# Attention scores in threes of adjoining PSUM banks, value products in cells of their own

## The reference, cut to what matters

```
x = x + linear_attention(_layernorm(x))   # 32 heads of 4, two decays, a scan over time, its own layer norm
x = x + ffn(_layernorm(x))                # 8 experts, all summed: silu(x @ wg) * (x @ wu) @ wd, 128 -> 512 -> 128
x = x + attention_b(_layernorm(x))        # 16 query heads of 8, one shared key/value head
x = x + ffn(_layernorm(x))                # the same weights again
```

```
att = einsum("bthd,bThd->bhtT", q, k) / sqrt(8)        # q, k after rotary tables
att = softmax(where(causal, -inf, att)); out = einsum("bhtT,bThd->bthd", att, v) @ Wo + bo
```

## Time and profile before

| | us |
|---|---|
| median of 3 runs | 1720.9 |
| the three runs | 1719.17, 1725.13, 1720.90 |
| the profiled execution | 1716.45 |
| its span | 1714.7 |

### The profile page before, as it was taken

The page is one execution under the profiler, slowest core; times in us unless marked ns, Lnnn a source line. Parts: engine busy times, 40 slices in busy tenths (PEclk is TensorE's granted clock), DMA queues, the critical chain, the costliest instruction groups (busy, mean ns, idle before and its releaser), DMA issues.

```text
span 1714.7 us, 24047 instructions
## 1 busy us (share of the span) xinstructions
PE 1574.8 (92%) x7848; PEld 1136.2 (66%) x7848; DVE 1169.0 (68%) x1943; ACT 892.6 (52%) x1552; POOL 723.4 (42%) x663
## 2 busy tenths in 40 slices
PE   3488998899999999899999999999999999999998
PEld 2266777677767676675665766767667667576676
DVE  5678787878787869676674755746647557466465
ACT  2255555464646464546445564464554644645554
POOL 3647354534444434311033544444344444343365
PEclk9689999999999999999999999999999999999999
DMA  6314543333334434333222332422323323333353
GB/s 196 111 41 162 192 160 115 148 135 144 127 148 148 148 119 147 140 111 111 111 101 85 126 128 85 146 102 107 138 92 130 117 107 115 118 111 117 111 191 117
DMA packets 36239, 216.71 MB, mean 126 GB/s; under 512 B 3475, under 2 KB 17300, under 8 KB 19732
## 3 DMA queue, kind: packets, MB, share of 16 engines
q1 hardware_dynamic: 36116, 215.18, 34.7%
HBM read 200.49 MB, written 15.47 MB: 126 GB/s over the span
## 4 chain that ended last, share of the span: by engine, by line
issue 29%; POOL 20%; PE 1%; POOLq 0%; DVE 0%; ACT 0%; DVEq 0%
POOL HL L525 18%; POOL QK L597 1%; POOL X L588 0%; POOL RSTD_f L516 0%; POOL RSTD_in L516 0%; POOLq L190 0%; PE bank L855 0%; PE bank L857 0%; PE bank L856 0%; POOL VE_f L513 0%; POOL VE_in L513 0%; POOL NB_in L520 0%; POOL NM_f L518 0%; POOLq L196 0%; POOL NM_in L518 0%
## 5 line engine op out<-in xcount | busy, mean ns | idle before, releaser
L525 POOL TENSOR_TENSOR HL<-HF,HH 128x512 fp32r<-128x512 f32 x312 | 417.4, 1338 | 657.7 <-ACT HH L689 657.7
L1233 DVE TENSOR_TENSOR HF<-SG,bank 128x512 f32<-128x512 f32 x512 | 349.5, 683 | 172.7 <-PE bank L857 103.6
L855 PE MATMUL bank<-XTH,W 128*128 128x512 f32 x1024 | 434.4, 424 | 10.4 <-ACT SG L682 9.9
L857 PE MATMUL bank<-XTH,W 128*128 128x512 f32 x1024 | 403.8, 394 | 0.0
L1216 DVE SCALAR_TENSOR_TENSOR SG<-SG,bank 128x512 f32<-128x512 f32 x288 | 197.9, 687 | 301.3 <-ACT SG L684 300.6
L856 PE MATMUL bank<-XTL,W 128*128 128x512 f32 x1024 | 403.1, 394 | 0.0
L684 ACT ACTIVATE SG<-bank 128x512 f32<-128x512 f32 x288 | 172.3, 598 | 399.4 <-PE bank L857 397.8
L689 ACT ACTIVATE HH<-HF 128x512 fp32r<-128x512 f32 x512 | 319.7, 624 | 28.4 <-DVE HF L1233 27.6
L682 ACT ACTIVATE SG<-bank 128x512 f32<-128x512 f32 x224 | 133.6, 596 | 245.7 <-PE bank L857 244.4
L855 PEld LDWEIGHTS bank<-XTH,W 128*128 128x128 f32 x1024 | 194.8, 190 | 91.6 <-issue 29.8
L855 PE MATMUL bank<-HH,W 128*128 128x512 f32 x512 | 216.8, 423 | 14.6 <-DVE HL L1222 13.4
(11 more groups left out here) (237 smaller groups left out, 1850.0 us busy)
## 6 DMA issues: line engine op xcount, KB each, us to landing
W<-kept_w SPq DMA_DIRECT2D x120, 1536.0 KB, 6.5
kept_w<-W SPq DMA_DIRECT2D x8, 1536.0 KB, 6.2
X<-in_L_attn_a_x_dram SPq DMA_DIRECT2D x8, 256.0 KB, 5.5
WS<-in_L_ffn_Wg_dram SPq DMA_DIRECT2D x8, 256.0 KB, 6.5
WS<-in_L_ffn_Wu_dram SPq DMA_DIRECT2D x8, 256.0 KB, 6.8
WS<-in_L_ffn_Wd_dram SPq DMA_DIRECT2D x8, 256.0 KB, 7.2
out_dram<-X SPq DMA_DIRECT2D x8, 256.0 KB, 7.2
CST<-in_tables_dram SPq DMA_DIRECT2D x1, 896.5 KB, 5.2
```

Source lines behind the costliest of these rows:

```text
L525: g.tensor_tensor(HL[:, n % HRING, :], HF[:, n % HFRING, :], HH[:, n % HRING, :].bitcast(F32), ALU.subtract).then_inc(F.hl, 1)
L855: pe.matmul(dst, wh, xh, start=start, stop=False)
L857: return pe.matmul(dst, wl, xh, start=False, stop=stop)
L1233: v.tensor_tensor(HF[:, n % HFRING, :], gated, fbank[(2 * n + 1) % 3], ALU.mult).then_inc(F.mul, 1)
```

## The change

The four side banks are now `three` (0, 1, 2, adjoining) and `abank` (3). The twelve units of scores of a sequence (a part and a group each; part 0 is the 128 by 128 block of all four heads of a group, parts 1 and 2 are 128 by 256 for two heads each) are taken in four threes, for rows as for columns; each unit fills one bank, so no bank is written by two row groups in one visit and `B.half` goes. A tile has 16 visits for 24, at alternating points 0 and 2. One Exp covers 1536 columns; PT holds the twelve banks of one sequence. The maxima are still six reductions a sequence, now of 512 to 1536 columns. Value products of a half are one cell with both parts. The FFN's ring of three banks is as it was. On ScalarE the Exp stands right behind the tanh, ahead of the HH copy; on VectorE maxima of visits at point 2 stand ahead of the doubled gate of the next slot. Cells of attention B get other slots and banks; its norm, turn and bias start five slots earlier, and statistics are at r = -21.

```diff
-ROW_PAIRS = [(0, 1), (2, 3), (4, 6), (5, 7), (8, 10), (9, 11)]
-PT_RING = 8
-B_CELL = {"turn": (-13, 1, 2), "q": (-8, 1, 0), "qs": (-8, 2, 1), "k": (-7, 1, 2), "ks": (-7, 2, 0), "v": (-5, 1, 0),
+B_CELL = {"turn": (-18, 1, 3), "q": (-8, 2, 0), "qs": (-7, 1, 1), "k": (-7, 2, 2), "ks": (-6, 1, 0), "v": (-5, 1, 1),
           "qst0": (-3, 1, 0), "qst1": (-3, 2, 1), "qst2": (-2, 1, 2), "qst3": (-2, 2, 0), "kst": (-1, 1, 1),
-          ("stack", 0, 0): (8, 1, 2), ("stack", 0, 1): (9, 1, 2), ("stack", 1, 0): (14, 1, 2),
-          ("stack", 1, 1): (15, 1, 2), ("sums", 0, 0): (20, 1, 2), ("sums", 0, 1): (21, 1, 2),
-          ("ot", 0): (22, 1, 2), ("out", 0): (23, 1, 2), ("sums", 1, 0): (27, 1, 2), ("sums", 1, 1): (27, 2, 1),
-          ("ot", 1): (28, 1, 2), ("out", 1): (29, 1, 2), "fturn": (33, 2, 2)}
-ROWS_AT = [[6 * b + i for i in range(6)] for b in range(SPT)]
-COLS_AT = [[12 + 6 * b + i for i in range(6)] for b in range(SPT)]
+          ("stack", 0, 0): (7, 1, 3), ("stack", 0, 1): (9, 1, 3), ("stack", 1, 0): (13, 1, 3),
+          ("stack", 1, 1): (15, 1, 3), ("pv", 0, 0): (16, 2, 3), ("pv", 0, 1): (18, 1, 3), ("sums", 0, 0): (20, 1, 3),
+          ("sums", 0, 1): (21, 1, 3), ("pv", 1, 0): (22, 2, 3), ("pv", 1, 1): (24, 1, 3), ("ot", 0): (25, 1, 3),
+          ("sums", 1, 0): (26, 1, 3), ("out", 0): (27, 2, 2), ("sums", 1, 1): (27, 1, 3), ("ot", 1): (28, 1, 3),
+          ("out", 1): (29, 1, 3), "fturn": (33, 1, 3)}
+ROWS_AT = [[(0, 2), (2, 0), (3, 2), (5, 0)], [(6, 2), (8, 0), (9, 2), (11, 0)]]
+COLS_AT = [[(12, 2), (14, 0), (15, 2), (17, 0)], [(18, 2), (20, 0), (21, 2), (23, 0)]]
+THREES = [[(0, 0), (0, 1), (0, 2)], [(0, 3), (1, 0), (1, 1)], [(1, 2), (1, 3), (2, 0)], [(2, 1), (2, 2), (2, 3)]]
+MAXIMA = [1, 3, 5, 6]
...
-            def exps(n, i):
-                m = 6 * n + i
-                act.wait_ge(B.t_ready, m + 1)
-                if m >= PT_RING // 2:
-                    act.wait_ge(B.pv, pv_of(m - PT_RING // 2))
-                act.activation(PT[:, at:at + 2, :], pair, ACT.Exp, scale=DB ** -0.5).then_inc(B.t_used, 1)
+                act.wait_ge(B.t_ready, 4 * n + i + 1)
+                after(act, B.pv, 2 * n)
+                act.activation(PT[:, 3 * i:3 * i + 3, :], three, ACT.Exp, scale=DB ** -0.5).then_inc(B.t_used, 1)
...
+                for at in range(0, 2 * SEQ, P):
+                    for x, (part, g) in enumerate(THREES[i]):
+                        if part == 0:
+                            pe.matmul(three[:, x, at:at + P], q[g][:, at // P, 0:P], ks[g][:, 0:P], start=(at == 0),
+                                      stop=False, skip_group_check=True)
+                        elif at % SEQ == 0:
+                            pe.matmul(three[:, x, at:at + SEQ], q[g][:, 2 * (part - 1) + at // SEQ, P:SEQ], ks[g],
+                                      start=(at == 0), stop=False, skip_group_check=True)
...
             def cols(t, b, i):
...
+                for x, (part, g) in enumerate(THREES[i]):
+                    rg = slice(g * RG, (g + 1) * RG)
+                    key = KST[rg, b * SEQ + P:(b + 1) * SEQ] if part == 0 else KST[rg, b * SEQ:b * SEQ + P]
+                    q2 = Q2[rg, b, :, P:SEQ] if part == 0 else Q2[rg, b, 2 * (part - 1):2 * part, :]
+                    pe.matmul(three[:, x, :], key, q2, start=True, stop=False, skip_group_check=True)
+                for x, (part, g) in enumerate(THREES[i]):
...
+            def values(n, b, z, dst):
+                pe.wait_ge(B.t_used, 4 * n + z + 3)
+                for g in range(NG):
+                    pe.matmul(dst[g * RG:(g + 1) * RG, :], VF[:, 2 * b, :], PT[:, NG * (z + 1) + g, :],
+                              start=True, stop=False, skip_group_check=True)
+                for g in range(NG):
+                    x = pe.matmul(r3(dst[g * RG:(g + 1) * RG, :], 2)[:, :, P:SEQ], VF[:, 2 * b + 1, :],
+                                  r3(PT[:, g, z * SEQ:(z + 1) * SEQ], 2), start=False, stop=True,
                                   skip_group_check=True)
...
+            def maxima(n, b, i):
...
+                for part in range(3):
+                    gs = [g for at, g in THREES[i] if at == part]
...
+                    v.tensor_reduce(dst, src, AX.X, ALU.max, negate=True).then_inc(B.row_used, 1)
...
+                new_maxima(slot, 2)
                 if n is not None and n >= TANH:
                     gated_half(n)
-                for t, r in b_tiles(slot):
-                    for b in range(SPT):
-                        if r in ROWS_AT[b]:
-                            maxima(t, b, ROWS_AT[b].index(r))
+                new_maxima(slot, 0)
```

More of the change, by code:

```diff
@@ L157, in side_cells, with put @@
     found = {}
[L159 to L162, removed]
+    def put(g, point, key):
+        bank = bank_of(key)
+        for at in range(3) if bank is None else (bank,):
+            assert (g, point, at) not in found, (g, point, at, key)
+            found[g, point, at] = key
     for t in range(NT):
[L164 to L167, removed]
+        for name, (r, point, _) in A_CELL.items():
+            put(a_slot(t) + r, point, ("a", t, name))
+        for name, (r, point, _) in B_CELL.items():
+            put(b_slot(t) + r, point, ("b", t, name))
@@ L830, in _ @@
                     gate_act(n)
+                for t, r in b_tiles(slot):
+                    for b in range(SPT):
+                        for i, (at, point) in enumerate(COLS_AT[b]):
+                            if r == at + (point == 2):
+                                exps(SPT * t + b, i)
                 n = unit_of(slot - 1)
@@ L970, in rows @@
                     pe.wait_ge(B.st_used, NJ * (t + 1))
[L971 to L978, removed]
-                                      stop=False, skip_group_check=True)
-                    for x in range(2):
-                        m = pe.matmul(r3(pair[:, x, :], NJ), MASKB[:, 2, :], spread(MASKB[:, 0, :], NJ), start=False,
-                                      stop=True, skip_group_check=True)
-                else:
-                    half = (units[0] - NG) % 2
-                    for j in range(2):
-                        for x in range(2):
-                            pe.matmul(pair[:, x, j * SEQ:(j + 1) * SEQ], q[x][:, 2 * half + j, P:SEQ], ks[x],
-                                      start=(j == 0), stop=False, skip_group_check=True)
-                    for x in range(2):
-                        m = pe.matmul(r3(pair[:, x, :], 2)[:, :, P:SEQ], MASKB[:, 2, :], spread(MASKB[:, 0, :], 2),
@@ L991, in rows @@
+                for x, (part, g) in enumerate(THREES[i]):
+                    if part == 0:
+                        m = pe.matmul(r3(three[:, x, :], NJ), MASKB[:, 2, :], spread(MASKB[:, 0, :], NJ),
+                                      start=False, stop=True, skip_group_check=True)
+                    else:
+                        m = pe.matmul(r3(three[:, x, :], 2)[:, :, P:SEQ], MASKB[:, 2, :], spread(MASKB[:, 0, :], 2),
                                       start=False, stop=True, skip_group_check=True)
@@ new lines, in cols @@
+                for x, (part, g) in enumerate(THREES[i]):
+                    if part == 0:
+                        m = pe.matmul(r3(three[:, x, :], NJ), MASKB[:, 2, :], spread(MASKB[:, 1, :], NJ),
+                                      start=False, stop=True, skip_group_check=True)
+                    else:
+                        m = pe.matmul(r3(three[:, x, :], 2)[:, :, 0:P], MASKB[:, 2, :], spread(MASKB[:, 1, :], 2),
+                                      start=False, stop=True, skip_group_check=True)
```

220 lines of the change are left out of this document (96 added, 124 removed).

## The result

The changed kernel takes 1668.84 us (median of 4 runs, 1668.22 to 1669.56) against 1720.04 us before (1717.51 to 1725.13): a ratio of 0.9699 with a 95% interval of [0.9676, 0.9722]. That is 51 us gained where the forecast was 25. The time lies inside the range, near its low end, in the part of it that belonged to rival 1. The profiled executions say the same: spans of 1714.7 and 1667.3 us, 47.4 apart.

What follows compares the result with a forecast made beforehand. TensorE (PE), 92% busy, was taken as the bound: 6.4 us a tile less work against 3.05 net new waits gave 20 for tiles 1 to 6, 3.35 for tile 7, 2 for tile 0; 25 us total, forecast 1695, range 1667 to 1713.

Steps and rivals of the forecast that it cites:

- rival 1: ScalarE and VectorE keep up, new waits do not come: 1680 us and below, 51 if only PE's sum counts; chance 0.22.
- PE's sum: TensorE's work for column visits, row visits and value products shrinks by 6.4 us a tile, 51 us over 8 tiles.
- the mixed visit: Second row visit, mixing 128- and 256-column matmuls on TensorE: between 1.14 and 1.36 us, taken as 1.25.
- the nearer row: Three row groups on TensorE taken to run together as two do in the trace.
- The old waits go: TensorE's waits for rope products ahead of ks and v, counted with record excess as 1.9 us a tile, disappear.
- 1.5 against 1.5: Tile 0: preparation moved into attention A's scans adds 1.5 us, losing its rope waits takes 1.5; 2 us gain left.
- The new waits: TensorE waits on ScalarE and VectorE at stacks, turn, value cells, second column visit and query stack: 4.95 us a tile.
- the stack (15,1): Stack cell sharing the turn's bank: TensorE there at 11.7, XL on VectorE done at 13.15, wait 1.5 us.
- the value cells: Value products at (16,2) and (22,2) wait for the Exp: 0.95 us, twice a tile.
- (13,1): Stack of sequence 1: TensorE there at 4.6, VectorE's split ends at 5.2, wait 0.6 us.
- Rival 2: Third row group does not run beside the other two, 0.21 us more a visit: 1712 to 1722 us; chance 0.12.
- Rival 3: Long Exp between tanh and HH holds the next tanh, FFN up waits: slower, 1747 us if wholly exposed; chance 0.07.

Runs made afterwards that it cites:

- experiment 6: Changed kernel with each half's value products in two cells again, the 256-column part one point later: 1679.07 us, ratio 0.9760.
- experiment 4: Changed kernel with the cells of q, qs, k, ks and v back in their old places: 1686.59 us, ratio 0.9816.
- experiment 5: Kernel before with only the new places of q, qs, k, ks and v, and one sums cell moved to another bank: 1698.04 us, ratio 0.9868.
- experiments 1 and 2: Changed kernel with each sequence's first value cell two FFN triples later: 1656.13 us; with the last stack cell also a slot later: 1650.03 us.
- experiment 3: Changed kernel with ScalarE's Exp behind the HH copy, as in the kernel before: 1680.71 us, ratio 0.9772.
- experiment 8: Changed kernel with VectorE's maxima of visits at point 2 behind the doubled gate: 1694.19 us, ratio 0.9849.

## Where the prediction held and where it failed, by its own steps

**PE's sum: right.** 6.68 us a tile by the busy row for 6.4. By visits: columns 3.95 for 3.96 a sequence, rows 4.24 for 4.38 (the mixed visit at its lower bound), a value product 0.35 saved for 0.29, which makes (1.69 + 1.10 + 0.70) x 2 = 7.0; with some 1.9 of old waits gone, 3.1 of new ones fill up to the 5.78 of the tile, about the 3.2 read above. All durations taken from "the nearer row" held, three row groups as two first of all. No run has the visits or the one value cell alone in the kernel before: these parts are read from times between starts, and experiment 6 bears out the value cell.

**The old waits go: right in the steady tile (1.74 by experiment 4 and 2.05 by experiment 5, for 1.9), wrong in tile 0.** There I wrote off 1.5 against 1.5 and left 2 us in all. The tile gained 6.75. The rope cells alone are 4.5 to 4.7 of that (experiments 4 and 5), because the waits there were 1.2 us each and the clock fell behind them. Both were in the trace before; I had read waits and clock of a steady tile alone. Tile 7 gained 4.2 for 3.35.

**The new waits: the step that failed.** The sentence "Sum 0.6 + 0.2 + 1.5 + 1.9 + 0.55 + 0.2 = 4.95 us a tile" had the places nearly all right and the size too large by 1.75: about 3.2 measured, of which the moves of experiments 1 and 2 took 2.70 away. Six tiles of 1.75 are 10.5 us. With 6 x 0.6 for PE's sum by visits, and 1.1 for the tile with the low clock, they are 15.2 of the 15.9 by which tiles 1 to 6 outdid their 20. Tile 0 adds 4.75 and tile 7 0.85. The 47.4 of the spans are then followed; the medians stand 51 apart, as the profiled execution of before lies 3.6 under the median of its four and that of the changed kernel 0.2 above its own. Forecast gain and measured gain of the spans, 25 and 47.4, are the fair pair.

Why too large? I had added up durations of records. ScalarE in slots 13 and 14 of the changed kernel, all in one row without an idle moment, and the split on VectorE that the stack (15,1) waits for:

```profile
1095.74 0.60 ACT L697 ACTIVATE SG<-bank 128x512 f32<-128x512 f32 x1 [1.95 <-PE bank L869]
1096.23 1.45 ACT L776 ACTIVATE PT<-three 128x1536 f32<-128x1536 f32 x1
1097.57 0.63 ACT L702 ACTIVATE HH<-HF 128x512 fp32r<-128x512 f32 x1
1098.08 0.60 ACT L811 ACTIVATE Q<-abank 128x512 fp32r<-128x512 f32 x1
1098.56 1.65 ACT L688 ACTIVATE XN<-X,NB_in,RSTD_in 128x128 f32<-128x128 f32 x4
1100.10 0.59 ACT L697 ACTIVATE SG<-bank 128x512 f32<-128x512 f32 x1
1100.58 1.46 ACT L776 ACTIVATE PT<-three 128x1536 f32<-128x1536 f32 x1
1101.91 0.64 ACT L702 ACTIVATE HH<-HF 128x512 fp32r<-128x512 f32 x1
1102.43 0.60 ACT L722 ACTIVATE XH<-abank 128x512 fp32r<-128x512 f32 x1
```
```profile
1103.07 0.69 DVE L1196 TENSOR_TENSOR XL<-abank,XH 128x512 fp32r<-128x512 f32 x1 [0.88 <-ACT XH L722]
```

The nine lines add up to 8.22 us. From the first start to the last end it is 1103.03 - 1095.74 = 7.29. A tanh of 0.60 is followed by the Exp after 0.49, an Exp of 1.45 by the copy after 1.34, a copy of 0.63 after 0.51. Each record outlasts its turn by about 0.11, and the end of a chain of nine is put 0.9 too late. For TensorE I had taken this into account (0.39 against 0.227) and for the other two not. The Trainium skill says it of this engine (ScalarE: Activation LUTs, What ACT_TABLE_LOAD costs): back-to-back ACTIVATEs overlap by about 93 ns. The trace has 0.10 to 0.14 us, the same thing somewhat larger.

Laid on the prediction's own scale (slot 12 starts at 1091.60), the split XL ends at 12.16, where the prediction has 13.15: 0.99 too late, of which the overlap is 0.93. But PE could have been at the stack at 11.28, where the prediction has 11.7, since the small waits ahead of it were overrated too. So the wait itself was overrated by less, 0.94 for 1.5. For the value cells the chain is two records long and the excess small: 0.83 for 0.95. For (13,1), behind VectorE's longest chain, it is 0.10 for 0.6. That chain has idle time in it, and how much of its excess is overlap was not worked out. For ScalarE's chain the cause is read from the records; no experiment changes the overlap, and for the waits as a whole it stays argued.

**Rival 1, the waits do not come**, gave the right time (1680 and below, and 51 us for "only the PE sum counts") and the wrong reason: the waits came, 3.2 us a tile, all but one at the places listed. That its 51 is the measured 51 is a coincidence. A gain of this size is the forecast's mechanism with a smaller term and a tile 0 that was left out. **Rival 2** did not happen. It was also priced at half: the 256-column rounds of one row group start 0.22 apart in the mixed visit above, so a third group wholly behind would add a pass of 0.44, not 0.21, and 16 x 0.44 = 7.0 us a tile would have made the kernel slower, not the same. **Rival 3** did not: no FFN `up` waits for the doubled gate, and where an Exp is held back (experiment 3) it is its own readers that PE meets.

**What would have made it slower** is closer than I thought, and lies on VectorE: experiment 8 costs half the gain by one swap.

## What to carry to other kernels

When you lay out what an engine will do between two cells, add up starts, not durations: take from the trace the spacing of the same instructions back to back, and the duration only for the last one of the chain. Read waits and granted clock in every stage that a change touches, the first tile too, since the clock that falls behind a wait can cost much of its length again (an estimated 1.7 us behind the 2.4 us of tile 0). And when a cell must read a long operation's result, see first whether its slot can move: here moving three cells by a slot or less brought 19 us, more than a third of what the whole change did.

## What the runs showed of the hardware that was not expected

- Records of ScalarE overlap back to back by 0.10 to 0.14 us, of VectorE by about 0.08 (a maximum of 1024 columns and one of 512 are 1.82 together and the next operation starts after 1.73).
- Three row groups of 32 rows run beside each other at no cost over two: 0.50 us for the group of two and of three. Groups with 128 and with 256 columns mix without one holding the other back, and their matmuls do not all start in the program's order.
- A 512-column fp32 matmul on a row group is a pass of 0.44 us (256-column rounds start 0.22 apart), against 0.227 for the fp32r matmuls of the FFN.
- To enter and leave one more cell of narrow tiles costs 0.33 to 0.36 us on TensorE (experiment 6), of which 0.10 is seen on the way in.
- Two waits of 1.2 us with 4.4 us of work between them were followed by the lower clock, 0.87 as the mean of ten microseconds; two of 0.8 in a steady tile were so in one tile out of six. With these waits gone, tile 0 had the full clock at that place.
